# One transformer block stack on one core: gathers of routed rows moved between two stages, and one memset moved ahead of them

## The chip, the core and the metric

The kernel runs on one core of a Trainium2 chip. Its time is the device time of one execution in microseconds (us). A core has five engines that run their own instruction streams and meet at semaphores: TensorE (PE, matrix products; its weight loads are listed as PEld), VectorE (DVE), ScalarE (ACT), GpSimd (POOL, which here also issues the indirect DMAs) and SyncE (SP, plain DMAs only). SBUF is the on-chip memory of 128 partitions, PSUM the accumulator banks of TensorE.

## The reference, cut to what matters

```python
x = L0_attn_hidden_states                      # (8, 256, 256) float32
x = x + _layernorm(_L0_attn_ref(_layernorm(x), ...))
x = x + _layernorm(_L0_ffn_ref(_layernorm(x), ...))   # 64 experts, top 4, and 2 shared ones
x = x + _layernorm(_L1_attn_ref(_layernorm(x), ...))  # chunked state-space layer
x = x + _layernorm(_L1_ffn_ref(_layernorm(x), ...))

# _L0_ffn_ref: each token's routed part is a sum over its four experts
routed = jnp.einsum('ne,nef,efd->nd', comb, g * u, wd)
# _L1_attn_ref begins with a projection and a causal convolution over 4 taps
proj = x @ W_in.T
val, gate, Bp, Cp, dt = jnp.split(proj, ...)
vc = conv_general_dilated(val, conv_w, (1,), [(D_CONV - 1, 0)], ...)
val = silu(vc + conv_b)
```

## The kernel before, in words

The 2048 tokens are 16 tiles of 128 tokens, in 4 chunks of 4 tiles (TPC is 4). Stages follow one another, each an own block of five instruction streams; all engines meet at the block's end, and none starts the next stage before the last of them has arrived. Two stages concern us.

**The expert stage, `stage_slots`.** Tokens have been scattered to 128 slot tiles by expert. They are worked through in 32 quads of 4 slot tiles, g = 0 to 31 (NQ is 32). For each quad TensorE turns the rows (L1478), multiplies up (L1500) and down (L1514); DVE copies one half of the turned rows (L1571), multiplies gate by up (L1598), and copies half of the previous quad's output from PSUM (L1605, ACT the other half at L1558), and SP stores it to `slots_out` in DRAM (L1452). In iteration g DVE does the copy of quad g+1, the product of quad g, the output copy of quad g-1. For quads from 16 on POOL and ACT also copy the weights of the expert that owns a slot (L1403, L1542), three quads ahead at most.

Chunk c's tokens lie in quads 0 to 19 + 4c (`quads_of`), so a chunk can be summed once these are stored (`stored(c)`). A gather (`fetch`, L1412) is one indirect DMA that POOL issues: it brings, for one tile of 128 tokens, the output row of one of its four experts (128 rows of 1 KB). Four gathers make a tile. `combine(i)` on DVE (L1580) adds the four, each times its share, to tile i of `y`. Before, POOL gathers two rows per quad from quad 24 on (EARLY_FROM, EARLY_EACH), and DVE sums chunk 0's four tiles in iterations 26, 28, 30 and 32 (COMBINE_AT). After the loop DVE takes the layer-norm statistics of `y` (L1585, then L436, L439, L440), POOL raises the variance to the power -0.5 (`deviations`, L1419), DVE adds the normed rows to `x` (L1614), takes the statistics of the new `x`, and POOL makes the powers of these. Between them POOL gathers the first two tiles of chunk 1, 24 gathers in all in this stage.

**The middle stage, `stage_mid`.** For chunk c = 0 to 3, ACT norms the rows (`normal_rows`, the helper's L453), TensorE turns them (L1785), ACT and DVE split them into a high and a low part (L1876, L1989), TensorE projects them in 9 blocks of 6 products (L1800), ACT takes each block out of PSUM (`take`: value blocks to `pad` and `conv`, L1888 and L1889, gate blocks to `gate`, L1897, the time steps to `z`, L1899), DVE convolves (L2001), ACT applies silu (L1909), TensorE turns the values (L1813), ACT copies them (L1914). `pad` holds three columns of zeros ahead of each sequence, set by POOL once (L1759); ACT waits for this (`padded`) ahead of its first `take`. TensorE has three PSUM banks for the blocks, so block 3 waits until ACT has taken block 0.

While chunk c is convolved, DVE sums, measures and adds chunk c+1: `combine` of two tiles at a time (L1964), statistics of y (L1975 and the helpers), the first two convolutions of chunk c, the addition to x (`add`, L1982, waits for POOL's power of y, L1750), statistics of x, the other two convolutions, and the low parts. ACT's `normal_rows(c+1)` waits for POOL's powers of x. POOL's stream is written out by hand: gathers of tiles 6 to 15 (four each, L1742, into a ring of 8 tiles), with the powers of chunks 1, 2 and 3 at fixed places among them. An instruction on POOL waits behind all that stand before it, gathers too.

## Time and profile before

| what | value |
|---|---|
| median of 3 runs | 1275.85 us |
| lowest and highest run | 1274.46 and 1279.34 us |
| the profiled execution, its time | 1269.8 us |
| its span (first to last instruction) | 1268.0 us |
| PE, DVE, ACT, POOL busy | 88%, 69%, 50%, 30% of the span |
| expert stage, with the quads after 16 | until 504.8 us of the span |
| middle stage | 504.8 to 631.0 us |

The profile is one execution on the chip; all times of day below are us from its start. Busy times count what an engine computes; a wait for a semaphore is idle time. In the timeline a row is one instruction or several alike in a row (x4), with the idle time of the engine before it in brackets and whose instruction ended that idle time. "issue" is time for which no releaser is seen; PEq and SPq are the sequencers of PE and SP.

### The profile page before, as it was taken

What the parts mean: (1) busy time and instruction counts of PE and PEld (TensorE: products, weight loads), DVE (VectorE), ACT (ScalarE), POOL (GpSimd) and SP (SyncE); (2) the same over time, 40 slices, a digit from 0 to 9 for tenths busy, and PEclk for the clock granted to TensorE, in tenths of its full rate; (3) what the DMA queues carried; (4) which work ended last, traced back from release to release, by engine and by line L of the source; (5) the groups of instructions that cost most, each with busy time, mean ns of one, the idle gap of its engine ahead of it and who ended that gap; (6) DMA issues with size and microseconds to landing.
All of it is one profiled execution on the core that took longest, in us unless ns stands there. A gap on an engine that the chain in (4) does not pass through costs nothing. (4 is left out here: it accounts for less than half of the span.)

```text
span 1268.0 us, 31644 instructions
## 1 busy us (share of the span) xinstructions
PE 1115.9 (88%) x12161; PEld 915.7 (72%) x12161; DVE 871.2 (69%) x2188; ACT 630.3 (50%) x1433; POOL 386.6 (30%) x561
## 2 busy tenths in 40 slices
PE   6569998689989993676799999999999999999987
PEld 5446776577778993455557888888888888888776
DVE  6467896877846776685476677667766776664574
ACT  4434456232333663476644554555455555553654
POOL 3331222176700265672055016202620261000120
PEclk9869999777999996777899999999999999999998
DMA  6748884222289885463243234223342332232001
GB/s 175 187 118 223 214 232 176 104 82 89 84 325 419 300 301 169 124 184 119 100 102 102 85 111 125 85 85 114 122 151 89 116 116 87 91 102 80 1 18 50
DMA packets 77986, 176.17 MB, mean 139 GB/s; under 512 B 12614, under 2 KB 26182, under 8 KB 75270
## 3 DMA queue, kind: packets, MB, share of 16 engines
q1 hardware_dynamic: 71564, 157.09, 38.6%
q0 software_dynamic: 6272, 17.05, 4.4%
q8 instruction: 97, 1.59, 0.5%
q14 instruction: 53, 0.43, 0.1%
HBM read 112.82 MB, written 61.08 MB: 137 GB/s over the span
## 5 line engine op out<-in xcount | busy, mean ns | idle before, releaser
L2378 ACT ACTIVATE decay<-masked,negcum 128x128 f32<-128x128 f32 x512 | 163.0, 391 | 101.8 <-DVE mixT L2442 101.8
L2286 PE MATMUL joint<-xh,w_high 128*128 128x512 f32 x512 | 209.3, 409 | 2.0 <-POOL wl L2222 2.0
L2286 PE MATMUL joint<-xl,w_high 128*128 128x512 f32 x512 | 200.2, 391 | 0.0
L2286 PE MATMUL joint<-xh,wl 128*128 128x512 f32 x512 | 199.9, 390 | 0.0
L2490 DVE COPY cT<-joint 128x512 f32<-128x512 f32 x128 | 88.3, 690 | 85.9 <-PE joint L2286 85.6
L2396 ACT ACTIVATE bT<-joint 128x512 f32<-128x512 f32 x128 | 76.7, 599 | 131.1 <-PE joint L2286 131.1
L2442 DVE TENSOR_TENSOR mixT<-pcb,decay 128x512 f32<-128x512 f32 x128 | 82.5, 685 | 55.7 <-PE pcb L2302 55.6
L2219 POOL TENSOR_TENSOR w_high<-w_in,none 128x512 fp32r<-128x512 f32 x32 | 36.1, 1127 | 260.7 <-DMA w_in<-in_w_bc 251.3
L2286 PEld LDWEIGHTS joint<-xh,w_high 128*128 128x128 f32 x512 | 96.2, 188 | 23.7 <-POOL wl L2222 2.4
L2286 PEld LDWEIGHTS joint<-xh,wl 128*128 128x128 f32 x512 | 96.1, 188 | 20.8
L2286 PEld LDWEIGHTS joint<-xl,w_high 128*128 128x128 f32 x512 | 96.3, 188 | 17.0
L2432 DVE TENSOR_TENSOR masked<-cumrow,mask 128x512 f32<-128x512 f32 x128 | 100.4, 784 | 0.0
L698 ACT ACTIVATE probT<-pst 128x384 f32<-128x384 f32 x128 | 60.4, 490 | 64.3 <-PE pst L629 61.0
L2302 PEld LDWEIGHTS pcb<-cT,bT 128*32 128x32 f32 x4096 | 79.5, 110 | 11.8 <-issue 11.6
L2302 PE MATMUL pcb<-cT,bT 128*32 128x128 f32 (+3 forms) x4096 | 84.9, 234 | 0.0
L968 POOL DMA_INDIRECT slots_in<-rows,slots x64 | 66.3, 1035 | 41.2 <-DMA slots_in<-rows,slots 20.3
L2451 DVE TENSOR_TENSOR cS<-cT,grown 128x256 f32<-128x256 f32 x128 | 62.3, 486 | 13.0 <-ACT grown L2383 1.3
L1598 DVE TENSOR_TENSOR rows<-gate,pgu 64x512 f32<-64x512 f32 x64 | 44.2, 691 | 27.7 <-ACT gate L1553 27.2
L739 DVE CUSTOM_DVE_ANT_0 masked<-ps,reach 128x256 f32<-128x256 f32 x128 | 53.8, 420 | 0.0
L737 DVE CUSTOM_DVE_ANT_0 masked<-ps,reach 128x128 f32<-128x128 f32 x128 | 36.8, 287 | 23.6 <-PE ps L613 22.4
L2383 ACT ACTIVATE grown<-cumrow 128x256 f32<-128x256 f32 x128 | 51.5, 403 | 0.0
L1742 POOL DMA_INDIRECT back<-slots_out,slots x40 | 42.6, 1066 | 15.3 <-issue 14.9
(367 smaller groups left out, 2717.3 us busy)
## 6 DMA issues: line engine op xcount, KB each, us to landing
cumrow<-ssm_cum SPq DMA_DIRECT2D x128, 256.0 KB, 3.2
slots_in<-blank SPq DMA_DIRECT2D x16, 1024.0 KB, 5.3
rows<-slots_in SPq DMA_DIRECT2D x32, 512.0 KB, 5.4
slots_out<-spare SPq DMA_DIRECT2D x32, 512.0 KB, 4.2
weights<-in_expert_quads SPq DMA_DIRECT2D x16, 768.0 KB, 8.8
w_in<-in_w_bc SPq DMA_DIRECT2D x32, 256.0 KB, 3.8
qk_parts<-parts SPq DMA_DIRECT2D x32, 192.0 KB, 2.3
stack<-qk_parts SPq DMA_DIRECT2D x32, 192.0 KB, 5.2
```

Of the source, the lines that this page charges most:

```text
L698: nc.scalar.activation(probT[:, n % HELD, :], pst[n % T_BANKS][:, 0:3 * P], ACT.Exp).then_inc(exped, 1)
L739: nc.vector.tensor_tensor_reduce(dst[:, P:3 * P], src[:, P:3 * P], reach[:], accum_out=highest[:, u % 2, j, 1:2], **form).then_inc(maxed, 1)
L968: nc.gpsimd.indirect_dma_start(out=xs[:, :], out_offset=bass.IndirectOffsetOnAxis(slots[:, i, k:k + 1], 0), in_=rows[:, i, :], in_offset=N ...
L2286: last = nc.tensor.matmul(bank[:], w[:, j, col:col + P], a[:, k, c * CHUNK:(c + 1) * CHUNK], start=(m == 0), stop=(m == len(parts) - 1))
L2302: last = nc.tensor.matmul(pcb[n % 2][at:at + KEY, reach], bT[:, n % B_BUFS, keys], cT[:, n % 2, reach], start=True, stop=True, skip_group_ ...
L2378: last = nc.scalar.activation(decay[:, n % 2, o], masked[:, n % 2, o], ACT.Exp, bias=negcum[:, c * TPC + i, head:head + 1])
L2383: nc.scalar.activation(grown[:, n % 2, :, :], row[:, :, P:S], ACT.Exp).then_inc(grown_out, 1)
L2396: nc.scalar.activation(bT[:, n % B_BUFS, :], pbT[:], ACT.Copy).then_inc(b_out, 1)
L2432: nc.vector.tensor_tensor(masked[:, n % 2, :].rearrange("p (q l) -> p q l", l=S), cumrow[:, n % CUMS, :].rearrange("p (q l) -> p q l", l=S ...
L2442: nc.vector.tensor_tensor(mixT[:, n % KEEP, :], pcb[n % 2][:], decay[:, n % 2, :], ALU.mult).then_inc(mix_out, 1)
L2451: nc.vector.tensor_tensor(cS[:, n % KEEP, :, :], second, grown[:, n % 2, :, :], ALU.mult).then_inc(c_scaled, 1)
L2490: nc.vector.tensor_copy(cT[:, n % 2, :], pcT[:]).then_inc(c_out, 1)
```

## The change

In the expert stage the gathers start at quad 23 instead of 24, so that two more are issued within the loop, and a wait for chunk 1's quads stands ahead of the first gather of chunk 1. DVE's four sums stand in iterations 25, 27, 29 and 31, and the statistics of y stand at the end of iteration 31, ahead of the last output copy. POOL has 6 gathers after its last weight copies instead of 8, four ahead of the power of y and two ahead of the power of x, none behind it. In the middle stage the zeros of `pad` are set ahead of all gathers, tiles 13 and 14 are gathered ahead of chunk 2's power of y, tile 15 ahead of its power of x; before, tile 13 stood between the two powers and tiles 14 and 15 behind both.

```diff
-EARLY_FROM, EARLY_EACH = 24, 2
+EARLY_FROM, EARLY_EACH = 23, 2
-COMBINE_AT = [26, 28, 30, 32]
+COMBINE_AT = [25, 27, 29, 31]
@@ stage_slots, POOL
                         for n in range((g - EARLY_FROM) * EARLY_EACH, (g - EARLY_FROM + 1) * EARLY_EACH):
+                            if n == TPC * TOPK:
+                                stored(1)
                             fetch(n)
-                for n in range((NQ - EARLY_FROM) * EARLY_EACH, TPC * TOPK):
-                    fetch(n)
                 pool.wait_ge(w_copied[1], OVER // 2)
                 link(nc.gpsimd.memset(norms["power"], -0.5))
-                stored(1)
-                late = list(range(TPC * TOPK, EARLY_TILES * TOPK))
-                for n in late[:4]:
+                for n in range((NQ - EARLY_FROM) * EARLY_EACH, EARLY_TILES * TOPK - 2):
                     fetch(n)
                 deviations(OF_Y)
-                for n in late[4:6]:
+                for n in range(EARLY_TILES * TOPK - 2, EARLY_TILES * TOPK):
                     fetch(n)
                 deviations(OF_X)
-                for n in late[6:]:
-                    fetch(n)
@@ stage_slots, DVE
                     if g in COMBINE_AT:
                         combine(COMBINE_AT.index(g))
-                for part in w_copied:
-                    dve.wait_ge(part, OVER // 2)
-                dve.wait_ge(added, TPC * TOPK)
-                statistics(y, OF_Y)
+                    if g == NQ - 1:
+                        for part in w_copied:
+                            dve.wait_ge(part, OVER // 2)
+                        dve.wait_ge(added, TPC * TOPK)
+                        statistics(y, OF_Y)
@@ stage_mid, POOL
+                nc.gpsimd.memset(pad[:, :, :, 0:TAPS - 1], 0.0).then_inc(padded, 1)
                 for i in range(EARLY_TILES, 9):
                     fetch(i)
                 link(nc.gpsimd.memset(power[:], -0.5))
-                nc.gpsimd.memset(pad[:, :, :, 0:TAPS - 1], 0.0).then_inc(padded, 1)
                 deviations(OF_Y, 1)
                 fetch(9)
                 deviations(OF_X, 1)
-                for i in range(10, 13):
+                for i in range(10, 15):
                     fetch(i)
                 deviations(OF_Y, 2)
-                fetch(13)
+                fetch(15)
                 deviations(OF_X, 2)
-                for i in range(14, NT):
-                    fetch(i)
```

Three places show what moved. Lines from the expert stage on are four or more lower in the changed file. First, POOL at the end of the expert stage, before; `spare` is where the gathered rows of tiles 0 to 5 lie, `weights` holds the small norm arrays.

```order
L1435 MEMSET weights 128x4 [waits raw_high_112]
L1412 DMA spare<-slots_out,slots 128x256 [waits y_scaled_103,y_spread_102,shift_loaded_84]
L1412 DMA spare<-slots_out,slots 128x256 x3
L1419 TENSOR_TENSOR weights<-weights 128x4 [waits scored_85]
L1422 TENSOR_TENSOR weights<-weights 128x4 [waits maxed_86]
L1412 DMA spare<-slots_out,slots 128x256 x2
L1419 TENSOR_TENSOR weights<-weights 128x4 [waits scored_85]
L1422 TENSOR_TENSOR weights<-weights 128x4 [waits maxed_86]
L1412 DMA spare<-slots_out,slots 128x256 x2
L1389 UNCONDITIONAL_BRANCH
```

And the same place after the change:

```order
L1412 DMA spare<-slots_out,slots 128x256 [waits y_scaled_103,y_spread_102]
L1412 DMA spare<-slots_out,slots 128x256
L1435 MEMSET weights 128x4 [waits raw_high_112]
L1412 DMA spare<-slots_out,slots 128x256 [waits shift_loaded_84]
L1412 DMA spare<-slots_out,slots 128x256 x3
L1419 TENSOR_TENSOR weights<-weights 128x4 [waits scored_85]
L1422 TENSOR_TENSOR weights<-weights 128x4 [waits maxed_86]
L1412 DMA spare<-slots_out,slots 128x256 x2
L1419 TENSOR_TENSOR weights<-weights 128x4 [waits scored_85]
L1422 TENSOR_TENSOR weights<-weights 128x4 [waits maxed_86]
L1389 UNCONDITIONAL_BRANCH
```

The last two gathers behind the second pair of powers are gone from the end; two more stand among the quads.

Second, DVE at the end of the expert stage, before, from the last product on; `fetched_22` is the semaphore of tile 3's gathers.

```order
L1598 TENSOR_TENSOR rows<-gate,pgu_199 64x512
L1605 COPY spare<-py_201 128x4x128 [waits y_spread_102,raw_loaded_110]
L1605 COPY spare<-py_203 128x4x128 [waits y_scaled_103,raw_loaded_110]
L1580 SCALAR_TENSOR_TENSOR y<-spare,share,y 128x256 [waits fetched_22]
L1580 SCALAR_TENSOR_TENSOR y<-spare,share,y 128x256 [waits ones_set_82] x3
L1585 BN_STATS weights<-y 128x6 [waits ones_set_82,raw_high_112,raw_loaded_111]
L1585 BN_STATS weights<-y 128x6 x3
```

The same place after the change:

```order
L1594 TENSOR_TENSOR rows<-gate,pgu_199 64x512
L1601 COPY spare<-py_201 128x4x128 [waits y_spread_102,raw_loaded_110]
L1576 SCALAR_TENSOR_TENSOR y<-spare,share,y 128x256 [waits fetched_22]
L1576 SCALAR_TENSOR_TENSOR y<-spare,share,y 128x256 [waits ones_set_82] x3
L1581 BN_STATS weights<-y 128x6 [waits ones_set_82,raw_high_112,raw_loaded_111]
L1581 BN_STATS weights<-y 128x6 x3
L436 BN_AGGR weights<-weights 128x2 [waits shift_loaded_83]
L436 BN_AGGR weights<-weights 128x2 x3
L439 TENSOR_SCALAR weights<-weights 128x4 [waits shift_loaded_83]
L440 TENSOR_SCALAR weights<-weights 128x4
L1601 COPY spare<-py_203 128x4x128 [waits y_scaled_103,raw_loaded_110]
```

The sum of tile 3 and the statistics of y now stand ahead of the last quad's output copy.

Third, POOL in the middle stage, before; `back` is the ring, x12 are twelve gathers, three tiles.

```order
L1742 DMA back<-slots_out,slots 128x256 x12
L1758 MEMSET norm_power 128x4
L1759 MEMSET pad 128x8x3 [waits x_in_39]
L1750 TENSOR_TENSOR norm_rstd<-norm_var,norm_power 128x4 [waits x_in_40]
L1753 TENSOR_TENSOR norm_shift<-norm_negmean,norm_rstd 128x4 [waits norm_chain_41]
L1742 DMA back<-slots_out,slots 128x256 x4
L1750 TENSOR_TENSOR norm_rstd<-norm_var,norm_power 128x4 [waits x_in_40]
L1753 TENSOR_TENSOR norm_shift<-norm_negmean,norm_rstd 128x4 [waits norm_chain_41]
L1742 DMA back<-slots_out,slots 128x256 x12
L1750 TENSOR_TENSOR norm_rstd<-norm_var,norm_power 128x4 [waits x_in_40]
L1753 TENSOR_TENSOR norm_shift<-norm_negmean,norm_rstd 128x4 [waits norm_chain_41]
L1742 DMA back<-slots_out,slots 128x256 x4
```

The same place after the change:

```order
L1753 MEMSET pad 128x8x3
L1739 DMA back<-slots_out,slots 128x256 x12
L1756 MEMSET norm_power 128x4
L1747 TENSOR_TENSOR norm_rstd<-norm_var,norm_power 128x4 [waits x_in_40,x_in_39]
L1750 TENSOR_TENSOR norm_shift<-norm_negmean,norm_rstd 128x4 [waits norm_chain_41]
L1739 DMA back<-slots_out,slots 128x256 x4
L1747 TENSOR_TENSOR norm_rstd<-norm_var,norm_power 128x4 [waits x_in_40]
L1750 TENSOR_TENSOR norm_shift<-norm_negmean,norm_rstd 128x4 [waits norm_chain_41]
L1739 DMA back<-slots_out,slots 128x256 x16
L1739 DMA back<-slots_out,slots 128x256 [waits x_in_37]
L1739 DMA back<-slots_out,slots 128x256 x3
L1747 TENSOR_TENSOR norm_rstd<-norm_var,norm_power 128x4 [waits x_in_40]
```

The zeros are first; ahead of chunk 2's power of y stand 20 gathers behind chunk 1's powers, where 12 stood.

## Rows read from the trace of the kernel before

**Rows 1.** Stretches: busy us (instructions) by engine, then the clock granted, DMA share, GB/s:
```profile
505.00:524.00 19.00, 8.18 (x26) 6.00 (x26) 11.80 (x26) 5.54 (x12) 13.96 (x14) 0.68 0.42 122
```

**Rows 2.** Waits, 500 to 600 us: who waited for whom, us in total, times, longest:
```profile
DVE y L1964 <- DMA back<-slots_out,slots: 14.0, 3, 6.5
...
ACT pad L1888 <- POOL pad L1759: 12.8, 1, 12.8
```

**Rows 3.** Timeline, DVE, expert stage: start, us, work [idle before <-releaser]:
```profile
459.88 1.39 DVE L1598 TENSOR_TENSOR rows<-gate,pgu 64x512 f32<-64x512 f32 x2 [1.19 <-ACT gate L1553]
...
463.78 1.39 DVE L1598 TENSOR_TENSOR rows<-gate,pgu 64x512 f32<-64x512 f32 x2 [1.19 <-ACT gate L1553]
...
471.86 1.39 DVE L1598 TENSOR_TENSOR rows<-gate,pgu 64x512 f32<-64x512 f32 x2 [0.41 <-ACT gate L1553]
```

**Rows 4.** Timeline of all engines, end of the expert stage:
```profile
484.41 1.39 DVE L1598 TENSOR_TENSOR rows<-gate,pgu 64x512 f32<-64x512 f32 x2
...
488.63 2.05 DVE L1580 SCALAR_TENSOR_TENSOR y<-spare,share,y 128x256 f32<-128x256 f32 x4
...
493.00 1.05 POOL L1419 TENSOR_TENSOR weights<-weights 128x4 f32<-128x4 f32 x1 [7.42 <-DVE weights L440]
...
498.00 1.05 POOL L1419 TENSOR_TENSOR weights<-weights 128x4 f32<-128x4 f32 x1 [1.24 <-DVE weights L440]
...
500.79 0.96 POOL L1412 DMA_INDIRECT spare<-slots_out,slots  x1 [0.30 <-issue]
...
504.81 0.33 SPq L1710 DMA_DIRECT2D tri<-in_tri  x1
```

**Rows 5.** Waits of SP's queue at the end of the expert stage:
```profile
SPq L1389 <- PEq L1389: 10.8, 1, 10.8
```

**Rows 6.** Timeline of all engines, start of the middle stage:
```profile
519.10 3.25 DVE L1964 SCALAR_TENSOR_TENSOR y<-back,share,y 128x256 f32<-128x256 f32 x8 [6.48 <-DMA back<-slots_out,slots]
...
522.95 0.12 POOL L1759 MEMSET pad<- 128x24 f32 x1
...
524.48 0.80 PE L1800 MATMUL pin<-xh,win_high 128*128 128x512 f32 x1 [8.81 <-ACT conv L1889]
...
526.10 4.07 DVE L2001 SCALAR_TENSOR_TENSOR conv<-pad,chan,conv 128x512 f32<-128x512 f32 x6 [1.62 <-ACT conv L1889]
```

**Rows 7.** Timeline, POOL, chunks 1 and 2 of the middle stage:
```profile
535.93 1.33 POOL L1742 DMA_INDIRECT back<-slots_out,slots  x1 [0.16 <-issue]
...
537.57 0.96 POOL L1742 DMA_INDIRECT back<-slots_out,slots  x1 [0.31 <-issue]
...
550.26 0.94 POOL L1742 DMA_INDIRECT back<-slots_out,slots  x1 [0.31 <-issue]
...
553.72 1.47 POOL L1750 TENSOR_TENSOR norm_rstd<-norm_var,norm_power 128x4 f32<-128x4 f32 x1 [2.52 <-DVE norm_var L440]
...
561.40 1.48 POOL L1750 TENSOR_TENSOR norm_rstd<-norm_var,norm_power 128x4 f32<-128x4 f32 x1
```

**Rows 8.** Timeline, DVE and its waits for gathers:
```profile
557.52 1.66 DVE L1982 SCALAR_TENSOR_TENSOR x<-y,norm_rstd,x 128x256 f32<-128x256 f32 x4
...
567.91 3.25 DVE L1964 SCALAR_TENSOR_TENSOR y<-back,share,y 128x256 f32<-128x256 f32 x8
...
576.85 3.26 DVE L1964 SCALAR_TENSOR_TENSOR y<-back,share,y 128x256 f32<-128x256 f32 x8 [5.70 <-DMA back<-slots_out,slots]
```

**Rows 9.** Timeline, ACT, norms of chunks 2 and 3, silu between:
```profile
563.39 2.08 ACT L453 ACTIVATE y<-x,norm_shift,norm_rstd 128x256 f32<-128x256 f32 x4 [1.76 <-POOL norm_shift L1753]
...
585.58 1.29 ACT L1909 ACTIVATE valT<-conv 128x512 f32<-128x512 f32 x2 [2.04 <-DVE conv L2001]
...
591.99 2.08 ACT L453 ACTIVATE y<-x,norm_shift,norm_rstd 128x256 f32<-128x256 f32 x4 [3.13 <-POOL norm_shift L1753]
```

**Rows 10.** Stretches with the projections of chunks 2 and 3, columns as in Rows 1:
```profile
569.40:582.90 13.50, 13.42 (x56) 10.73 (x55) 7.70 (x25) 9.84 (x19) 4.34 (x5) 0.93 0.53 168
...
598.00:606.60 8.60, 8.60 (x42) 6.82 (x42) 1.00 (x2) 5.59 (x11) 0.00 (x0) 0.77 0.22 88
```

## The prediction

> **What bounds the kernel now.** TensorE is busy for 88% of the whole span, but the page's chain of waits names only the last few per cent of the program, so I went to the stretch that is edited. I read three views: busy time by stretch, where TensorE works for only 8.18 of the 19 us from 505 to 524 and its granted clock averages 0.68 [rows 1]; the list of waits over the middle stage, where two entries stand out, ACT held for 12.8 us by POOL's zeros of `pad`, and DVE held for 14.0 us in three waits by the landing of gathers [rows 2]; and the timelines, for who is last at each hand-over. They say that in both stages the end is set by a ring of DVE, POOL and ACT, with TensorE waiting. I count times of the middle stage from its first instruction, 504.81 [rows 4], and write them m+.
>
> **The end of the expert stage.** DVE's product for the last quad starts at 484.41; then come two output copies, and only at 488.63 the sum of tile 3. The power of y starts at 493.00, that of x at 498.00, and behind it POOL issues the last two gathers, the second from 500.79 to 501.75. The next stage begins at 504.81, 3.06 after that [rows 4]. SP had been at the barrier for 10.8 us, since 494.0 [rows 5].
>
> Moving the sums one quad earlier costs the quads little: a quad without a sum takes 3.90 (459.88 to 463.78), and two quads with one sum between take 8.08 (463.78 to 471.86), not 7.80 [rows 3]. There are three such pairs before and after, and the fourth sum moves from behind the last quad into it. There, sum 3 follows the product and one copy: 484.41 + 1.39 + 0.69 gives about 486.5 instead of 488.63, so 2.1 are saved. Sum 2 no longer stands right ahead of the last product either, worth 0.4 as I judge it (the product then waits for its silu, where it waited for the sum). I take 2.5 and bound it by 1.5 and 2.9. The last copy, 0.7, now lies behind the statistics, while POOL works on the power for 1.05; nothing. The powers of y and x come 2.5 earlier, that of x at 495.5, ending with its product (1.3) at 496.8. The two gathers behind it are gone; they stand among the quads, where POOL has room. So POOL leaves at 496.8, not 501.75: 5.0 earlier. SP's last store waits for the moved copy: about 2.4 later than before, so SP is ready at about 496.4. It is just not last. The barrier's 3.06 was paid behind a gather; behind a small tensor product, for which no row stands, it may be shorter, so I keep 3.06 and take half of it, 1.5, as a bound of what more there is. **Term 1: -5.0** (bounds -2.5, if SP's store ends the stage, and -2.9 - 2.4 - 1.5 = -6.8).
>
> **Chunk 0 of the middle stage.** The zeros are set at 522.95, behind 12 gathers, and ACT and then TensorE (8.81 idle) wait for them [rows 6]. Ahead of the gathers they are ready at m+1, costing the gathers 0.15. ACT then takes blocks as TensorE makes them, and the projection ends some 11 us earlier. But DVE doesn't get its inputs earlier: its sum of tiles 6 and 7 still starts when the gathers land, at 519.10 or m+14.3, and the statistics end at m+19.7. Only the 1.62 that DVE then waited for ACT's `conv` ahead of the first convolution goes [rows 6]. **So of the 12.8 only 1.62 - 0.15 = 1.5 reach DVE**, and with it chunk 1's power of x. TensorE's cleared 8.81 becomes waiting for the convolution and the norms of chunk 1.
>
> **Chunk 1 and the gathers moved.** Behind chunk 1's powers POOL issues gathers from 535.93, m+31.1; in the changed kernel from m+29.65. Twelve of them start 1.303 apart (535.93 to 550.26 is 11 intervals) [rows 7]. Before, POOL was through at 551.20 and idle for 2.52 until DVE had chunk 2's variance; its power began at 553.72, m+48.9 [rows 7]. Now there are 20: m+29.65 + 19 x 1.303 + 0.94 = m+55.35. The power of y is 6.4 late against the stage's start. Its result was used at 557.52 [rows 8], 2.3 after it was ready at 555.19, so DVE's addition is 4.1 late. Tile 15's four gathers follow, as tile 13's did, and the power of x comes 7.68 after that of y as before (553.72 to 561.40) [rows 7]: 6.4 late too, since DVE's 4.1 is less. ACT's norms of chunk 2, before at 563.39 (m+58.6) right on the power's product [rows 9], come at m+65.0.
>
> **What is given back in chunk 2.** DVE's sum of tiles 12 and 13 started at 567.91, and that of 14 and 15 waited 5.70 for gathers, to 576.85 [rows 8]. Now all have landed by then. The first sum moves from m+63.1 to m+69.5, the second follows at once, at m+72.8 instead of m+72.0: 0.7 late. On ACT's side, the projection of chunk 2 and the taking of its blocks are 6.4 late; behind them stood 2.04 of waiting ahead of the silu and 3.13 ahead of the norms of chunk 3 [rows 9], together 5.2, so 1.2 stay over. The later of the two counts. **Term 2: +1.2**, bounds -0.8 and +3.2 from the gather interval (the ten intervals from 537.57 to 550.26 average 1.27 [rows 7], which would take 0.6 off; as much above as 1.38 would put 1.5 on) and from the clock: TensorE now idles for some 20 us with only transposes between the projections of chunk 1 and 2. In the projection of chunk 2 the granted clock averaged 0.93 over 13.5 us, in that of chunk 3, after a longer stretch of waiting, 0.77 over 8.6 [rows 10]; with half and full speed as the two levels that is 1.9 and 4.0 us at half. If chunk 2's starts like chunk 3's, that adds (4.0 - 1.9) / 2 = 1.0; chunk 3's, with less idle ahead of it than before, may give the same back. I take nothing for the clock. The Trainium skill ("TensorE: Matmul & The Clock Gate", Part 4: PE-mode transpose) says that transposes do not count as work for the clock. By that rule chunk 2's projection starts at half speed, and the sum would be 1.0 less gain; the row of chunk 3 agrees with it and no row refutes it.
>
> From m+88 on nothing differs. Sum: -5.0 + 1.2 = **-3.8 us**, against the profiled execution (1269.8, span 1268.0): 1266.0. The median of the runs shown is 6 us above that execution, so I take the difference off the median: 1275.85 - 3.8 = **1272.0 us**.
>
> **Rivals.**
>
> A, the forecast: 1272.0. For it: POOL's stream is in order, and 20 x 1.3 us of gathers don't fit into the 19 us or so that DVE leaves between chunk 1's power of x and chunk 2's variance. Chance 0.52.
>
> B, the hold is shorter than priced and the border gives more. If gathers run 1.27 apart (-0.6), the barrier behind a tensor product is 1.5 shorter, and chunk 3's projection gains 1.0 in clock: -3.8 - 3.1 = -6.9, 1268.9. For it: the intervals behind the first of a series are even; against it: it wants three small things at once, though each may be larger than I think. Chance 0.27.
>
> C, the expert stage ends as before or nearly, because SP's last store, now behind the moved copy, lands last: if it lands at 499 instead of 496.4, term 1 shrinks to 2.8 or less: 1274.3. For it: it waits on a copy that is 2.4 later, beside gathers; against: the load of the input weights, which ran beside it before, is over by then. Chance 0.12.
>
> D, slower: gathers are slowed when they are issued beside DVE's sums and convolutions. The price is on POOL between chunk 1's and chunk 2's powers: at the spacing of a series' first pair, 1.64 (535.93 to 537.57) [rows 7], 24 gathers take 24 x 0.34 = 8.1 us more, which the norms of chunk 2 pass on to the end: +4.3, 1280.2. It decides from a spacing of 1.303 + 3.8 / 24 = 1.46 on. For it: the power of 4 columns takes 1.05 at the end of the expert stage [rows 4] and 1.47 beside DVE's convolution [rows 7]. Against it: the twelve gathers averaged 1.303 with sums and statistics beside them. Chance 0.09. The Trainium skill ("SBUF — State Buffer", SBUF: two separate sides) has a rule that speaks for it: DVE and GpSimd share a pair of ports, locked for a whole instruction, and gathers' descriptors are written through it. The longer power agrees; the steady gathers do not.
>
> **How the numbers follow.** About 0.5%, 6.4 us, is what a measurement of this kernel can tell from no change. Faster by more than that, under 1269.5: nearly all of B short of its smaller half and a tenth of A, 0.27. Slower by more, over 1282.2: only the end of D and noise, 0.05. Between: 0.68. The range takes A and C with bounds, most of B: 1267.0 to 1277.5. For A alone it is 1270 to 1275.
>
> **What would show each step.** Zeros of `pad` within 1.5 us of the middle stage's start, and no wait of ACT on them. The middle stage begins at 499 to 500.5, and POOL's last instruction before it is the product behind the power of x. DVE's wait for the gathers of tiles 6 and 7 stays at 6 us or more. POOL issues 20 gathers in a row, and the power of chunk 2's y starts behind them with no idle time ahead of it; DVE's addition then waits some 4 us on POOL, where it waited for nothing. The wait of 5.7 for tiles 14 and 15 is gone. ACT's norms of chunk 2 start 65 us into the stage. The forecast is wrong if DVE reaches chunk 2's variance later than the gathers end, if the middle stage's length shrinks by more than 1 us or grows by more than 4, or if another engine is last at the first border.

## The result and the profile after

The changed kernel takes 1265.43 us (median of 13 runs, 1260.69 to 1271.40), the kernel before, run beside it, 1271.86 us (13 runs, 1269.07 to 1279.34). The ratio is 0.9945 with a 95% interval of 0.9924 to 0.9965, which is 7.0 us less (4.4 to 9.7). The forecast was 3.8 us less. Besides, its base, the 1275.85 us of three runs, lay 4 us above what 13 runs gave, so that the forecast time misses by 6.6 us and the difference by 3.2.

The span of the profiled execution, 1267.3 us, is hardly shorter than before's 1268.0. This execution came to the edited place 7.1 us later than that of before, with nothing changed ahead of it: POOL's weight copy of quad 23 starts at 452.50 against 445.43. Over all profiles taken here this start lies between 445.4 and 455.8. So I compare lengths, not times of day: **length 1** from that copy to the middle stage's first instruction, **length 2** from there to the stage's end. They are 59.42 and 126.21 us before, 53.35 and 124.65 after. From the stage's end to the span's end it is 636.9 and 636.8. Both lengths and the m+ of this part count from DVE's first instruction of the stage (504.85 and 505.85), 0.04 behind SP's, from which the prediction counted.

The changed kernel, timeline of all engines at the end of the expert stage (start, us, work, idle before), against [rows 4]:

```profile
490.68 1.40 DVE L1594 TENSOR_TENSOR rows<-gate,pgu 64x512 f32<-64x512 f32 x2
...
492.83 2.05 DVE L1576 SCALAR_TENSOR_TENSOR y<-spare,share,y 128x256 f32<-128x256 f32 x4
...
497.19 1.04 POOL L1419 TENSOR_TENSOR weights<-weights 128x4 f32<-128x4 f32 x1 [3.39 <-DVE weights L440]
...
502.19 1.05 POOL L1419 TENSOR_TENSOR weights<-weights 128x4 f32<-128x4 f32 x1 [1.24 <-DVE weights L440]
503.32 0.20 POOL L1422 TENSOR_TENSOR weights<-weights 128x4 f32<-128x4 f32 x1
505.81 0.33 SPq L1707 DMA_DIRECT2D tri<-in_tri  x1
```

From the last product to the last sum it is 2.15 us instead of 4.22, and POOL's last instruction is the small product, ended at 503.52. The next stage's first instruction comes 2.29 behind it, where before it came 3.06 behind a gather. SP's queue was not last, though its margin shrank from 10.8 us [rows 5]:

```profile
SPq L1389 <- PEq L1389: 4.0, 1, 4.0
```

The start of the middle stage after the change, stretch of the same place in the stage as [rows 1] (us, busy by engine PE, PEld, DVE, ACT, POOL, clock, DMA share, GB/s):

```profile
506.05:525.05 19.00, 16.57 (x61) 13.19 (x62) 11.38 (x23) 12.12 (x22) 13.65 (x14) 0.74 0.56 160
```

Waits after the change, 501 to 601 us, against [rows 2]; ACT no longer waits for POOL's zeros, but for TensorE's blocks, and DVE waits for gathers twice, not three times:

```profile
DVE y L1959 <- DMA back<-slots_out,slots: 12.7, 2, 6.9
...
ACT pad L1883 <- PE pin L1795: 9.5, 11, 2.3
```

Timeline of POOL after the change, against [rows 6, 7]: the zeros first, then 20 gathers in a row and the power of chunk 2's y behind them with no idle time.

```profile
506.06 0.12 POOL L1753 MEMSET pad<- 128x24 f32 x1 [2.54 <-POOLq L1389]
...
535.80 1.33 POOL L1739 DMA_INDIRECT back<-slots_out,slots  x1 [0.16 <-issue]
537.44 0.97 POOL L1739 DMA_INDIRECT back<-slots_out,slots  x1 [0.30 <-issue]
...
561.01 0.95 POOL L1739 DMA_INDIRECT back<-slots_out,slots  x1 [0.31 <-issue]
561.98 1.05 POOL L1747 TENSOR_TENSOR norm_rstd<-norm_var,norm_power 128x4 f32<-128x4 f32 x1
```

Timeline of DVE and ACT after, against [rows 6, 8, 9]: the sum of tiles 6 and 7, the addition, the sum of four tiles, and the norms of chunks 2 and 3.

```profile
520.55 3.26 DVE L1959 SCALAR_TENSOR_TENSOR y<-back,share,y 128x256 f32<-128x256 f32 x8 [6.95 <-DMA back<-slots_out,slots]
...
563.06 1.70 DVE L1977 SCALAR_TENSOR_TENSOR x<-y,norm_rstd,x 128x256 f32<-128x256 f32 x4 [4.43 <-POOL norm_rstd L1747]
...
570.29 2.08 ACT L453 ACTIVATE y<-x,norm_shift,norm_rstd 128x256 f32<-128x256 f32 x4 [9.65 <-POOL norm_shift L1750]
...
574.81 6.41 DVE L1959 SCALAR_TENSOR_TENSOR y<-back,share,y 128x256 f32<-128x256 f32 x16
...
593.93 2.07 ACT L453 ACTIVATE y<-x,norm_shift,norm_rstd 128x256 f32<-128x256 f32 x4
```

The middle stage starts at 505.85, so these are the norms of chunk 2 at m+64.4 and those of chunk 3 at m+88.1 (before m+58.6 and m+87.1). The stretch from the norms of chunk 3 to the stage's end I call the **tail**: 36.57 us after, 39.07 before. Stretches with the projections of chunks 2 and 3 after, against [rows 10]:

```profile
576.30:589.80 13.50, 13.50 (x52) 11.02 (x52) 12.63 (x34) 9.47 (x18) 1.38 (x2) 0.84 0.29 113
600.00:608.60 8.60, 8.60 (x47) 6.97 (x46) 2.32 (x4) 6.35 (x13) 0.00 (x0) 0.93 0.22 86
```

In this execution the two have changed places: chunk 2's projection starts at m+70.5 and has 0.84 of the full clock (0.93 before), chunk 3's 0.93 (0.77 before). The slower one is felt on DVE, which before went from chunk 3's statistics to chunk 2's convolution without a wait:

```profile
584.09 4.07 DVE L1996 SCALAR_TENSOR_TENSOR conv<-pad,chan,conv 128x512 f32<-128x512 f32 x6 [0.73 <-ACT conv L1884]
```

ACT takes these blocks as TensorE makes them.

### The profile page after: what moved, and what is told of

Its sections match the earlier page's. It is cut to its first block and busy times, and to the rows that moved or that the text cites. A ratio compares the mean times of both kernels' runs of the same rounds, so it can differ in the third digit from the quotient of the medians.

```text
span 1267.3 us, 31645 instructions
## 1 busy us (share of the span) xinstructions
PE 1114.0 (88%) x12161; PEld 914.5 (72%) x12161; DVE 869.7 (69%) x2188; ACT 630.5 (50%) x1433; POOL 387.9 (31%) x561
## 3 DMA queue, kind: packets, MB, share of 16 engines
q1 hardware_dynamic: 71564, 157.09, 38.8%
## 5 line engine op out<-in xcount | busy, mean ns | idle before, releaser
L2485 DVE COPY cT<-joint 128x512 f32<-128x512 f32 x128 | 88.3, 690 | 85.7 <-PE joint L2281 85.4
L2437 DVE TENSOR_TENSOR mixT<-pcb,decay 128x512 f32<-128x512 f32 x128 | 82.4, 685 | 55.8 <-PE pcb L2297 55.7
L2229 POOL COPY y<-val 32x128 f32<-32x128 f32 x128 | 43.7, 341 | 7.6
```

The lines of the kernel that those rows point to most:

```text
L2437: nc.vector.tensor_tensor(mixT[:, n % KEEP, :], pcb[n % 2][:], decay[:, n % 2, :], ALU.mult).then_inc(mix_out, 1)
L2485: nc.vector.tensor_copy(cT[:, n % 2, :], pcT[:]).then_inc(c_out, 1)
```

## The experiments

All values of a table row are from that kernel's one profiled execution; m+ counts from the stage's first instruction. "Sum" is the start of DVE's sum of tiles 10 and 11. "Half" is TensorE's time at 1.2 GHz in the tail: the sum, over stretches of the tail, of (1 - granted clock) x 2 x length. "Sum 14" is the start of DVE's sum of tiles 14 and 15, and "wait" what DVE then waits for ACT's `conv` ahead of chunk 2's first convolution.

| kernel | length 1 | sum | sum 14 | wait | norms 3 | tail | half | length 2 |
|---|---|---|---|---|---|---|---|---|
| before | 59.42 | 43.40 | 72.00 | 0 | 87.14 | 39.07 | 16.9 | 126.21 |
| e1, e11 (before) | 58.38, 58.44 | 43.52, 43.41 | 72.04, 72.29 | 0, 0 | 87.18, 87.42 | 39.20, 38.35 | 17.1, 15.9 | 126.38, 125.77 |
| changed | 53.35 | 43.38 | 72.12 | 0.73 | 88.08 | 36.57 | 10.2 | 124.65 |
| e5, e12 (changed) | 53.15, 53.08 | 43.62, 42.91 | 72.36, 72.19 | 0.55, 0 | 88.13, 87.32 | 37.69, 37.90 | 13.7, 13.6 | 125.82, 125.22 |
| e2, e14 border only | 53.37, 52.86 | 44.17, 44.68 | 72.36, 73.18 | 0, 0 | 87.49, 88.32 | 38.08, 37.91 | 15.4, 15.2 | 125.57, 126.23 |
| e3, e13 zeros only | 59.40, 58.53 | 42.66, 42.67 | 71.37, 71.18 | 0, 0 | 86.50, 86.32 | 36.51, 37.30 | 10.7, 14.3 | 123.01, 123.62 |
| e4 gathers only | 59.09 | 43.91 | 73.20 | 0 | 88.32 | 38.03 | 13.6 | 126.35 |
| e6 without gather move | 53.07 | 43.48 | 71.96 | 0 | 87.10 | 37.54 | 14.8 | 124.64 |
| e8 two gathers last | 55.99 | 43.77 | 72.46 | 0.66 | 88.34 | 36.53 | 10.3 | 124.87 |
| e7 split 16/3/5 | 53.40 | 42.89 | 69.34 | 0 | 84.47 | 37.60 | 14.9 | 122.07 |
| e9 split 16/4/4 | 53.09 | 43.09 | 68.33 | 0 | 83.46 | 37.88 | 13.8 | 121.34 |
| e10 + products, all chunks | 53.03 | 43.11 | 67.70 | 0 | 82.84 | 35.89 | 6.9 | 118.73 |
| e16 + products, last chunk | 53.20 | 44.34 | 70.76 | 0 | 85.90 | 34.82 | 3.5 | 120.72 |
| e15 before + products | 58.60 | 45.61 | 74.10 | 0 | 89.24 | 34.75 | 3.5 | 123.99 |

In every row the norms of chunk 3 start 15.1 us behind "sum 14", and later by about the wait where there is one (88.08 - 72.12 = 15.96 in the changed kernel).

### The parts of the change, each alone

**Before once more**, no edit.

> The kernel before once more, for one thing: how much the two lengths that the argument uses move from execution to execution. Length 1 is from POOL's first weight copy for quad 23 to the middle stage's first instruction (59.4 us in the trace of before, 53.3 in that of the changed kernel), length 2 the middle stage (126.2 and 124.7). If the gain is the edit's, both come out as in the first trace, within 0.3 for length 1 and within 1.5 for length 2, whose projections start at half clock for a time that varies. Rival: the stage lengths scatter by several us as the whole time does (1269 to 1279), and then one pair of traces shows nothing.

Measured: 1275.23 us; lengths 58.38 and 126.38. Length 2 came as expected, length 1 moved by 1.0, not 0.3. The lengths of one kernel repeat within about a microsecond, its whole time does not; every later reading goes by lengths.

**Border only**: the expert stage of the changed kernel, the middle stage of before.

> Only the expert stage's part of the change (gathers from quad 23, sums in iterations 25 to 31, statistics in iteration 31, no gather behind the powers of x); the middle stage as before. Theory: length 1 falls from 59.4 to 53.3 and length 2 stays at 126.2 within 1.5. Rival: part of length 1 comes from the zeros standing first in the next stage (first instruction sooner), so that length 1 is 54.5 or more.

Measured: 1264.23 us in one run; length 1 is 53.37. Length 2, 125.57, is as expected. The part of the change that carries term 1 stands alone. End of the expert stage:

```profile
497.97 0.20 POOL L1422 TENSOR_TENSOR weights<-weights 128x4 f32<-128x4 f32 x1
500.45 0.33 SPq L1707 DMA_DIRECT2D tri<-in_tri  x1
```

**Zeros only**:

```diff
+                nc.gpsimd.memset(pad[:, :, :, 0:TAPS - 1], 0.0).then_inc(padded, 1)
                 for i in range(EARLY_TILES, 9):
                     fetch(i)
                 link(nc.gpsimd.memset(power[:], -0.5))
-                nc.gpsimd.memset(pad[:, :, :, 0:TAPS - 1], 0.0).then_inc(padded, 1)
```

> Only the zeros of pad ahead of the gathers. Theory: ACT and TensorE lose their 12.8 and 8.8 us of waiting, but DVE goes on waiting for the gathers of tiles 6 and 7, so only the 1.5 us ahead of the first convolution reach the end: length 2 is 124.7, give or take 1 for the clock. Rival 1: TensorE's 8.8 us reach the end, length 2 is 118 to 120. Rival 2: nothing reaches it, since DVE's wait for tiles 14 and 15 takes it up: 126.2, with that wait grown from 5.7 to 7.2.

Measured: 1269.87 us in one run. Chunk 1's power of x is 1.5 us earlier (m+27.6, before m+29.1), the norms of chunk 3 only 0.65, and the tail is 2.6 shorter. Length 2 is 123.01, less than the theory's 124.7 give or take 1; rival 1's 118 to 120 and rival 2's 126.2 did not come.

**Gathers only**: 20 and 4 gathers ahead of chunk 2's powers, as in the changed kernel, all else as before.

> Only the gathers of the middle stage moved: 20 instead of 12 ahead of chunk 2's power of y, tile 15 ahead of its power of x; zeros late as before, expert stage as before. Theory: the power of y starts behind the gathers at 57.5 us into the stage (48.9 before), ACT's norms of chunk 2 at 66 (58.6 before), the wait of 5.7 for tiles 14 and 15 goes, and the sum is a loss of 2 us: length 2 is 128.2, give or take 1.5 for the clock. Rival: the wait that goes is worth more than the hold, length 2 is under 126.

Measured: 1277.22 us in one run. The power of y comes at m+57.2, the norms of chunk 2 at m+65.5, those of chunk 3 at m+88.3: 1.1 later than before. Length 2 is 126.35, as before, and neither the 128.2 (give or take 1.5) of the theory nor under the rival's 126: the loss was overrated.

### Is the gain real, and whose is it

**The changed kernel again**, timed.

> The changed kernel once more, profiled and timed beside the two others of this call. Length 1 and the middle stage up to ACT's norms of chunk 3 come out as in its first trace (53.35, and 88.1 us into the stage) within 0.3. From there on, how long TensorE's projection of chunk 3 and the sums behind it run at half clock decides: theory, this varies from execution to execution or with small shifts of the schedule, so length 2 lies anywhere from 124.3 to 127.5. Rival: it is fixed by the order of work, then 124.65 again. Timed: 0.993 to 0.997 of the kernel before.

Measured: 1265.77 us against 1273.87, ratio 0.9942 (0.9925 to 0.9959). The result repeats, with length 2 at 125.82 instead of 124.65, so it is not fixed by the order of work.

**Without the gather move**: the changed kernel with tiles 13, 14 and 15 gathered where they were before.

> The changed kernel with the middle stage's gathers put back in the old order (12, 4 and 8 around chunk 2's powers); expert stage and zeros stay changed. Theory: the moved gathers cost more than they save, 88.1 - 86.5 = 1.6 us at ACT's norms of chunk 3, so these start at 86.5 us into the stage, and the kernel is 1.6 us faster than the changed one, 0.991 to 0.995 of the kernel before. Rival, the idea behind the move: the 5.7 us of waiting for tiles 14 and 15 that come back cost more than the hold, and it is slower than the changed kernel by 1 us or more.

Measured: 1266.0 us, ratio 0.9942 (0.9918 to 0.9966). Norms of chunk 3 at m+87.1, 1.0 earlier than in the changed kernel and not 1.6; the medians don't tell the two apart.

**Two gathers back behind the last power** at the end of the expert stage, all else changed:

```diff
-                for n in range(EARLY_TILES * TOPK - 2, EARLY_TILES * TOPK):
-                    fetch(n)
                 deviations(OF_X)
+                for n in range(EARLY_TILES * TOPK - 2, EARLY_TILES * TOPK):
+                    fetch(n)
```

> The changed kernel with the last two gathers of the expert stage put back behind the powers of x. Theory: POOL leaves the stage 2.4 us later, and the border costs 3.1 behind a gather instead of 2.3 behind a small tensor product, together 3.2: length 1 is 56.5 (53.35 in the changed kernel, 59.4 before). Rival: the border's cost has nothing to do with the last instruction's kind, and length 1 is 55.8; or SP's last store ends the stage soon after POOL and part of it is covered, length 1 under 55.5.

Measured: 1267.66 us in one run; length 1 is 55.99, 2.8 above the 53.2 without it. That length alone lies nearer the rival's 55.8 than the theory's 56.5; what decides is the border itself. POOL at the end of the stage, and the next stage's first instruction:

```profile
499.06 0.20 POOL L1422 TENSOR_TENSOR weights<-weights 128x4 f32<-128x4 f32 x1
499.42 1.02 POOL L1412 DMA_INDIRECT spare<-slots_out,slots  x1 [0.15 <-issue]
500.74 0.96 POOL L1412 DMA_INDIRECT spare<-slots_out,slots  x1 [0.30 <-issue]
504.72 0.33 SPq L1707 DMA_DIRECT2D tri<-in_tri  x1
```

It comes 3.02 behind the gather's end (501.70), against 2.28 behind the product in the border-only kernel (498.17 to 500.45). So the two gathers cost 2.4 of issue and about 0.75 at the border, less 0.5 by which the power of x, with no gathers ahead of it, came earlier (49.2 into length 1, 49.7 in the changed kernel).

### A better split

**16/3/5 and 16/4/4**: so many gathers of tiles 10 to 15 ahead of chunk 2's power of y, between it and that of x, and behind (before 12/4/8, changed 20/4/0). The core of the edit for 16/4/4:

```diff
-                for i in range(10, 15):
-                    fetch(i)
+                for n in range(10 * TOPK, 10 * TOPK + 16):
+                    gather(n)
                 deviations(OF_Y, 2)
-                fetch(15)
+                for n in range(10 * TOPK + 16, 10 * TOPK + 20):
+                    gather(n)
                 deviations(OF_X, 2)
+                for n in range(10 * TOPK + 20, NT * TOPK):
+                    gather(n)
```

> The changed kernel with the 24 gathers of tiles 10 to 15 cut otherwise: 16 ahead of chunk 2's power of y, 3 ahead of its power of x, 5 behind. Theory: the power of y then starts some 2.3 us behind the variance, which its user can bear; the power of x starts with the variance, at 56 us into the stage; and the last gathers land at 66.5, one us behind DVE's sum of tiles 12 and 13. So neither the hold (6 us) nor the wait (5.7) is paid: norms of chunk 3 start at 82.5 to 83.5 us into the stage (88.1 in the changed kernel), length 2 is 119 to 121.5, and the kernel is 4 to 5 us faster than the changed one: 0.988 to 0.992 of the kernel before. Rival: ACT or TensorE becomes the bound there (projection of chunk 2), and only half of it comes: norms of chunk 3 at 85 or later.

Measured: 1261.71 us, ratio 0.9910 (0.9883 to 0.9938). DVE's sum of tiles 14 and 15 and ACT's norms of chunk 3 (stage from 508.11), these at m+84.5, a microsecond behind the 82.5 to 83.5 expected and ahead of the rival's 85, with a wait for gathers of 3.16 that was not expected; length 2, 122.07, is 0.6 above its 119 to 121.5:

```profile
577.45 3.25 DVE L1966 SCALAR_TENSOR_TENSOR y<-back,share,y 128x256 f32<-128x256 f32 x8 [3.16 <-DMA back<-slots_out,slots]
...
592.58 2.08 ACT L453 ACTIVATE y<-x,norm_shift,norm_rstd 128x256 f32<-128x256 f32 x4 [2.42 <-POOL norm_shift L1754]
```

> Edit: as the changed kernel, but the gathers of tiles 10 to 15 are split 16 ahead of chunk 2's power of y, 4 between it and the power of x, and 4 behind it (the changed kernel has 20, 4, 0; the kernel of the last step 16, 3, 5). Nothing is left out of the computation. Theory (POOL's stream, in order, sets chunk 2's norms, and the landing of the last gathers sets chunk 3's sum): the fourth gather between the powers holds the power of x by up to 1.3 us, to about m+57.8, the sum of tiles 12 and 13 starts at about m+64.2, the wait for the last gathers is at most 1.5 us (3.16 with 16/3/5), and ACT's norms of chunk 3 start at m+83 to m+84. Median 3.8 to 5 us below the changed kernel, ratio to the kernel before 0.987 to 0.992. Rival (the hold and the wait cancel): norms of chunk 3 at m+84.5 or later, and a ratio no lower than that of 16/3/5, 0.991.

Measured: 1261.26 us, ratio 0.9912 (0.9890 to 0.9935). The same two rows (stage from 500.99):

```profile
569.32 3.26 DVE L1966 SCALAR_TENSOR_TENSOR y<-back,share,y 128x256 f32<-128x256 f32 x8 [0.61 <-DMA back<-slots_out,slots]
...
584.45 2.08 ACT L453 ACTIVATE y<-x,norm_shift,norm_rstd 128x256 f32<-128x256 f32 x4 [0.93 <-POOL norm_shift L1754]
```

The steps came as expected (power of x at m+58.0, wait 0.61, norms at m+83.5), and the median is 4.2 us below the changed kernel's; the microsecond gained over 16/3/5 does not show in the ratio, as the rival had it. Both beat the changed kernel by 4 us in median and 3 to 4 us in length 2, though the intervals of the ratios still touch its own: the hold of POOL is gone and most of the wait for the last gathers too.

### What makes the tail long or short

**Both kernels a third time**, no edit.

> Edit: none, the kernel before once more, one profiled execution. Twice its tail (from ACT's norms of chunk 3 to the end of the middle stage) was 39.1 and 39.2 us, with 12.9 and 13.3 us at half clock in m+91 to m+126. If the edit decides the tail, it is 38.8 to 39.5 again. If the tail merely varies between executions, it should come below 38.5 in one of three. The length to the middle stage should be 58.4 to 59.5 us, norms of chunk 3 at m+87.0 to m+87.3.

> Edit: none, the changed kernel once more, one profiled execution. Its tail was 36.6 and 37.7 us in two executions, with 7.6 and 11.2 us at half clock in m+91 to m+126. If the edit decides the tail, it is 36.4 to 37.9 again. If it merely varies between executions, a value above 38.5 should be as likely as not. Length to the middle stage 53.1 to 53.5 us, norms of chunk 3 at m+88.0 to m+88.3.

Measured: before 1269.13 us with a tail of 38.35, changed 1269.75 us with 37.90. The tail of before is under the 38.8 to 39.5 that was to mean that the edit decides it, and under the 38.5 that was to mean chance; that of the changed kernel is just within its 36.4 to 37.9. So both hold in part. The changed kernel's norms of chunk 3 came at m+87.3, 0.7 ahead of what was expected. Its sum of tiles 12 to 15 started as in the first execution (m+69.03 and m+68.96), but its projection of chunk 2 had 0.95 of the clock, not 0.84, and DVE did not wait for ACT's `conv`:

```profile
576.50:590.00 13.50, 13.14 (x56) 10.55 (x54) 13.36 (x36) 9.93 (x19) 1.88 (x2) 0.95 0.31 121
583.43 4.06 DVE L1996 SCALAR_TENSOR_TENSOR conv<-pad,chan,conv 128x512 f32<-128x512 f32 x6
```

With three each, the tail is 38.9 before and 37.4 after on average; the groups don't overlap, but they come within 0.5 of each other. Of the first execution's fast projection of chunk 3 nothing is left in the other two: over the whole projection the clock is 0.82, 0.82 and 0.83 in the three of before, 0.95, 0.82 and 0.83 in the three changed.

**Extra products in the wait ahead of the next norms**, on top of 16/4/4, in chunks 0 to 2:

```diff
                     values(c, (0, 1))
+                    pe.wait_ge(taken, (c + 1) * CB_IN)
+                    for _ in range(12):
+                        nc.tensor.matmul(pin[0][:], wh[:, 0, 0:P], xh[:, 0, bass.ts(c, CHUNK)], start=True, stop=True)
                     turn(c + 1)
```

> Edit: as 16/4/4, and in the middle stage TensorE makes 12 extra products of 128x512 per chunk (results unused, into the first of its three banks once that has been taken) between the turning of the first and the second pair of values, just ahead of where it waits for the next chunk's norms. So the kernel does 36 to 48 products more than the function needs. Theory (the tail from ACT's norms of chunk 3 to the end of the stage varies by TensorE's clock at the start of the projection, which follows on a stretch in which TensorE hardly works): the time at half clock from m+91 on falls from 7.6 to 13 us to at most 7, and the tail to 36.5 us or less, whatever the extra products do to the rest. They take 12 x 0.21 = 2.6 us at full clock or 5.1 at half, and lie in a wait of about 10 us, so norms of chunk 3 should not be later than in 16/4/4 by more than 0.5 us. Rival (the clock there does not depend on the work put into that wait, or the products run at half clock themselves and delay the turning): half-clock time over 9 us, or norms later by 1 us and more, and a median no better than 16/4/4.

Measured: 1263.37 us, ratio 0.9928 (0.9904 to 0.9951). As the theory had it, the tail is 35.9 and half-clock time 6.9, and the middle stage is 2.6 us shorter than in 16/4/4; the median is no better, as the rival had it. But in the profile the rest of the program took 641.2 us instead of 636.0 (the expectation of e16 counts this rest 0.1 to 0.3 shorter). Of these 5.2 us one standstill of TensorE in the next stage, with no releaser shown, makes 2.9; the others were not traced:

```profile
923.89 0.17 PEld L2307 LDWEIGHTS pcb<-cT,bT 128*32 128x32 f32 x9 [2.90 <-issue]
923.89 0.44 PE L2307 MATMUL pcb<-cT,bT 128*32 128x32 f32 x9 [2.63 <-issue]
```

**The same products, ahead of chunk 3's norms only** (`if c == TPC - 2`), in the kernel before:

> Edit: the kernel before, in which TensorE makes 12 extra products of 128x512 (results unused) between the turning of chunk 2's first and second pair of values, ahead of its wait for the norms of chunk 3. 12 products more than the function needs. Theory (half clock at the start of chunk 3's projection makes the tail long): half-clock time from the norms of chunk 3 to the stage's end falls from 15.9 to 17.1 us to under 12, the tail from 38.4 to 39.2 us to 36 to 37, norms of chunk 3 stay at m+87.1 to m+87.4; median 2 us below the kernel before. Rival (the tail is set by ACT and DVE, and the clock only goes along): half-clock time falls, the tail stays at 38 us or more.

Measured: 1270.8 us, ratio 0.9991 (0.9973 to 1.0009). The tail fell from 39 to 34.75, more than forecast, and half-clock time to 3.5; the median fell by 1.1 us (3.4 less to 1.1 more), where 2 were forecast. Stretch from the norms of chunk 3 to the stage's end, in the kernel before:

```profile
591.99:631.06 39.07, 29.69 (x140) 23.33 (x140) 16.52 (x25) 25.34 (x43) 2.11 (x4) 0.78 0.24 88
```

in the changed kernel:

```profile
593.93:630.50 36.57, 27.19 (x140) 21.44 (x140) 16.53 (x25) 25.23 (x44) 2.12 (x4) 0.86 0.26 98
```

and in the kernel before with the 12 products:

```profile
603.62:638.37 34.75, 25.05 (x140) 19.70 (x140) 16.51 (x25) 25.03 (x43) 2.12 (x4) 0.95 0.27 99
```

DVE and ACT do the same work in the same time in all three; TensorE's busy time falls as the clock rises, from 29.69 to 27.19 to 25.05, and the stretch from 39.07 to 36.57 to 34.75. So a faster TensorE shortens the tail, with DVE's and ACT's work unchanged, and the rival that these two set it falls. What TensorE did ahead of the projection of chunk 3 (16 transposes; 8 more follow), and the projection's first 10 us, in the kernel before:

```profile
583.00:596.40 13.40, 4.07 (x16) 3.00 (x16) 11.98 (x27) 6.80 (x13) 3.08 (x4) 0.57 0.15 58
598.06:608.06 10.00, 10.00 (x48) 7.96 (x47) 2.46 (x4) 6.59 (x13) 0.00 (x0) 0.80 0.19 73
```

and with the 12 products among the transposes:

```profile
597.00:608.00 11.00, 7.18 (x32) 5.63 (x32) 9.80 (x24) 6.57 (x12) 1.88 (x2) 0.84 0.13 48
608.54:618.54 10.00, 10.00 (x57) 8.19 (x56) 4.31 (x7) 8.38 (x16) 0.00 (x0) 1.00 0.26 102
```

The norms of chunk 3 came 2 us late, though, at m+89.2, which nobody expected. The cause lies ahead of the products: the gathers of tiles 10 and 11 landed late. DVE, stage from 514.38:

```profile
559.99 3.26 DVE L1968 SCALAR_TENSOR_TENSOR y<-back,share,y 128x256 f32<-128x256 f32 x8 [4.23 <-DMA back<-slots_out,slots]
```

**And on top of 16/4/4:**

> Edit: the split 16/4/4 with the same 12 extra products ahead of chunk 3's norms only. With them in all chunks the middle stage was 118.7 us instead of 121.3, but the rest of the program took 640.9 us where all others take 635.8 to 636.9, after a pause of TensorE of 2.9 us in the next stage. Theory (the pause is a matter of one execution or of where the instruction stream was longer, not of the clock): middle stage 119 to 120 us, tail 36 us, rest 636 to 637 us, and a median 1.5 us below 16/4/4, ratio 0.989 to 0.991. Rival (the products cost later what they gain here): rest over 638.5 us and a ratio of 0.992 or more.

Measured: 1261.44 us, ratio 0.9904 (0.9876 to 0.9931). Tail 34.8 (36 expected), middle stage 120.72 (119 to 120 expected), rest 637.0, so no pause behind the stage; the median is not the 1.5 us lower that was expected. But again the sum of tiles 10 and 11 started 1.2 later than in 16/4/4 and the norms of chunk 3 2.4 later. Whether the later norms come with the longer program or by chance in two executions stays open.

### What the timed parts add up to

> Edit: the kernel before with the zeros of pad set ahead of the gathers, nothing else; timed this time. Theory (the early zeros shorten the tail from the norms of chunk 3 to the stage's end, by way of TensorE's clock): tail 36.5 to 37.9 us, norms of chunk 3 at m+86.5 to m+87.2, middle stage 123 to 125 us against 125.8 to 126.4; median 1.5 to 2.5 us below the kernel before, ratio 0.998 to 0.999, which five rounds hardly tell from 1. Rival (the tail varies by itself between executions): tail over 38 us, and no difference in the median.

Measured: 1272.27 us, ratio 0.9999 (0.9984 to 1.0014). In the profile the stage is 2.5 us shorter than before's average of 126.12, but the medians show nothing (at most 2.0 less). So the profile's shorter stage, seen in both profiles of this kernel, is not borne out by the time, and I count the zeros at no more than 2 us. Tail and stage are as the theory had them, the median as its rival had it.

> Edit: the kernel before with the expert stage of the changed one (gathers from quad 23 on, sums one quad earlier, statistics ahead of the last copy, no gather behind the powers), middle stage as before; timed this time. Theory (the lengths of the profiles are what the median sees): length to the middle stage 53.0 to 53.5 us against 58.4 to 59.4, tail 38.0 to 39.2 us, median 5.2 to 6.2 us below the kernel before, ratio 0.995 to 0.996. Rival (the gain at the border is larger or smaller in the median than in the profiles, by contention that a profile disturbs): a ratio under 0.994 or over 0.997.

Measured: 1266.91 us, ratio 0.9948 (0.9929 to 0.9966), 6.6 us less (4.3 to 9.0). Length 1, 52.86, and the tail, 37.91, lie 0.1 under what was expected. **The border alone gives what the whole change gives.** The 6.6 is 0.4 us more than the 5.2 to 6.2 expected, and its interval holds the 5.6 of length 1.

## Why the prediction was wrong

Each step forecast up to chunk 2 showed in the trace, with sizes a little off. The clock was taken at nothing, and there the sum failed. By the averages of three profiles of each kernel: length 1 from 58.75 to 53.19, -5.6; norms of chunk 3 from m+87.25 to m+87.84, +0.6; tail from 38.87 to 37.39, -1.5. Sum -6.5, beside the -7.0 of the medians. The forecast had -5.0, +1.2 and 0, so the misses are 0.6, 0.6 and 1.5.

**Term 1, -5.0, measured -5.6.** POOL leaves 4.8 earlier (forecast 5.0). The border was kept at 3.06 and is 2.3 behind a small tensor instruction; e8 brings the 3.0 back by putting a gather last. The bound of 1.5 held it, but the sum was made with none of it. In medians the border part is -6.6 (e14). Rival C, SP's store ending the stage, did not come. The medians put more on the border than the lengths do, 6.6 of the 7.0, which leaves 0.4 for all the rest, with an interval of 2.4 either way: they can't tell how the miss is shared between the border and the clock.

**The zeros.** Right that only 1.5 of ACT's 12.8 reach chunk 1's power of x: it is 1.4 earlier on the average of three (m+29.13 to m+27.74). Right too that most of this reaches chunk 2: with 20/4/0 chunk 2's power of y starts at m+56.2 with early zeros (average of three) and at m+57.2 with late ones (e4). It does not reach DVE's sum of tiles 10 and 11. The last gather for it, the eighth behind that power, starts 0.8 earlier (m+40.25 to m+39.47), the sum 0.1 (m+43.44 to m+43.30): from its end to that sum a gather took 2.1 to 2.5 in the three of before and 2.7 to 3.1 in the three changed. That DMA carries more in this stretch now, since chunk 1's blocks and their stores run beside it, is my guess; no run isolates it. In the changed kernel nothing later shows a tie to this sum: the sum of tiles 12 to 15 starts 12.8 us behind chunk 2's power of y in all five profiles with 20/4/0, with this one anywhere from m+42.9 to m+43.9.

**The gather move, the rest of term 2.** The steps are right: the 20 gathers hold the power of y until m+56.1 (forecast 55.35; they came 1.33 apart, 535.80 to 561.01 in 19 intervals, not 1.303), the norms of chunk 2 come at m+64.4 (forecast 65.0), the wait for tiles 14 and 15 is gone. The sum of tiles 14 and 15 starts only 0.1 later than before on average (m+72.22 against m+72.11), where 0.7 was forecast. From it to the norms of chunk 3 it is 15.1 us in every profile without DVE's wait for ACT's `conv`. The changed kernel has this wait in two of three executions, 0.73 and 0.55 (and 0.66 in e8), where chunk 2's projection spent 4.4 and 3.9 us at half clock (4.2 in e8); in e12 and e4, with 1.3 and 1.5 us, there is none. That is the other 0.5 of the +0.6. So the cause that the forecast named and left out, chunk 2's projection starting slow, did cost something, though not in each execution. The bounds given for term 2, -0.8 and +3.2, don't come out of the terms named for them (-0.6 and -1.0 make +1.2 into -0.4, +1.5 and +1.0 into +3.7).

**"From m+88 on nothing differs", and "I take nothing for the clock": the step that failed, worth 1.5 us.** The instructions from there on are the same, but they don't take the same time. TensorE's time at half clock in the tail is 15.9 to 17.1 us before and 10.2 to 13.7 after, and e15, with 3.5, has a tail 4.3 us shorter. The prediction had read [rows 10] rightly and named both halves of the exchange: chunk 2's projection slower, chunk 3's faster. I let them cancel. They don't weigh the same. Chunk 2's projection lies beside DVE's chain of sum, statistics and convolution, which hid most of it: 2.6 us more at half clock in the first execution (4.4 against 1.8) made DVE wait 0.73. In the tail no such chain runs beside TensorE (DVE is busy 16.5 of 37 to 39 us), so half-clock time is paid there.

The Trainium skill ("TensorE: Matmul & The Clock Gate", Part 4: PE-mode transpose) says that transposes don't count as busy time of TensorE in the same way, so that the full clock does not come on. The traces agree: in all 15 profiles without extra products the projections of chunks 2 and 3, with only transposes ahead, start at half clock; with products among the transposes chunk 3's starts at the full one (e15, e16). They can't tell this from TensorE having less to do there (busy 4.07 of 13.40 us without products, 7.18 of 11.00 with them). And how long the half clock then lasts is not fixed by the kernel: 1.3 to 4.4 us for chunk 2 and 1.2 to 4.3 for chunk 3 in three executions of the changed one.

**Whether the change itself brings the faster clock is not settled.** The tail is 36.5 to 37.9 in the nine profiles with early zeros and no products, and 37.9 to 39.2 in the six without either. The zeros are set 83 to 88 us ahead of it and touch nothing in it. It also moves by 1.3 us between executions of one kernel. And e13 finds no time in the medians for it. So of the -1.5 the part that belongs to the change may be smaller than the three profiles say.

**Rivals.** B, -6.9, had the right size, in part by luck: the shorter border came (0.75 instead of 1.5) and chunk 3's clock (1.5 instead of 1.0), while the gathers' spacing went the other way, and the smaller cost at chunk 2 was not among its parts. D fell: 24 gathers beside DVE's work came 1.3 apart, far from 1.46.

## What to carry to other kernels

An in-order queue that both issues transfers and makes small results should have as many transfers ahead of each result as fit into the time until its input is there, counted in instructions and not in tiles: 16/4/4 is worth 4 us over 20/4/0, by the medians and by length 2, for no added work. At a stage's end let the last instruction of a queue be a plain one, with no transfer issued behind the result that the next stage waits for. Before writing that nothing differs from some place on, look at the clock in the rows at that place, set the stretch at the projection's own start (after the change, the same offset into the stage as before gives 0.62 where the projection has 0.84), and ask beside which of two stretches another engine's chain lies, and how much slack it has. One profile does not show what clock a kernel gets there; three did.

## What the runs showed of the hardware that I had not expected

- The border between two stages costs 2.3 us behind a small tensor instruction of POOL and 3.0 to 3.1 behind a gather (ten and eight profiles; e8 changes nothing else at the border).
- Twelve extra products in a wait bring the tail, with the same 140 products and transposes, from 39.07 to 34.75 us in the kernel before (e15) and from 37.88 to 34.82 in 16/4/4 (e16). In the median it brought nothing that can be measured; the norms ahead came later in both.
- One kernel with one and the same order of work gave chunk 2's projection 1.3, 3.9 and 4.4 us at half clock in three executions, and DVE's wait behind it was 0, 0.55 and 0.73.
- From the end of one and the same gather's issue to the sum that waits for it took 2.0 to 3.5 us over the 18 profiles.
- One execution (e10) lost 2.9 us to a standstill of TensorE some 300 us behind the edited stage; whether the added instructions cause it stays open, and e16, with fewer of them, doesn't show it.
